# A decoder layer on one core of Trainium2: second buffers for eleven tiles, dummy matmuls at the start, and new orders and banks

## The reference

```python
# attention with positive random features, 16 heads of 16, 64 features a head
q, k, v = (split(x @ W.T + b) for W, b in ((Wq, bq), (Wk, bk), (Wv, bv)))
phi = lambda a: (exp(a @ orf.T / 16**0.25 - sum(a*a, -1) / (2*sqrt(16))) + 1e-6) / sqrt(64)
kv, ksum = phi(k).T @ v, sum(phi(k), tokens)
att = (phi(q) @ kv) / (phi(q) @ ksum)              # merged heads @ Wo.T + bo
x1 = layernorm(x + att)
# cross attention: 16 heads of 16, softmax between the context and x1, weights shared by the heads
x2 = layernorm(x1 + cross_attention(x1, ctx, Wq, Wk, Wv))
# feed-forward layer 256 -> 1024 -> 256, 8-bit activations and ternary weights
h = gelu(bitlinear(x2, w_gate)) * bitlinear(x2, w_up)
out = layernorm(x2 + bitlinear(h, w_down))
```

## Time and profile before

| what | value |
|---|---|
| median of 3 runs | 495.16 us (495.1 to 498.17) |
| the profiled execution | 495.66 us, its span from the first to the last instruction 493.6 us |
| busy: TensorE, VectorE, ScalarE, GpSimd | 447.2, 436.0, 429.1, 393.3 us (91, 88, 87, 80%) |
| mean granted TensorE clock | 0.977 of full speed |
| one tile in the full loop, 258.02 to 270.95 | 12.93 us, TensorE busy 12.93, ScalarE 12.85, VectorE 12.72, GpSimd 12.07 |

### The profile page before, as it was taken

The page is one execution under the profiler, slowest core; times in us unless marked ns, Lnnn a source line. Parts: engine busy times, 40 slices in busy tenths (PEclk is TensorE's granted clock), DMA queues, the critical chain, the costliest instruction groups (busy, mean ns, idle before and its releaser), DMA issues.

```text
span 493.6 us, 18532 instructions
## 1 busy us (share of the span) xinstructions
PE 447.2 (91%) x6598; PEld 305.1 (62%) x6598; DVE 436.0 (88%) x1286; ACT 429.1 (87%) x879; POOL 393.3 (80%) x885
## 2 busy tenths in 40 slices
PE   5588898999999999999999999999999999878752
PEld 3345666777666766777767677766766666554321
DVE  7755568999999999999999999999999999898771
ACT  3398988999999999999999999999999999776632
POOL 3379677889997898999999999999999897764533
PEclk9889999999999999999999999999999999997997
DMA  7848667777787587566666666666667676542122
GB/s 206 263 109 140 124 120 110 132 134 140 142 142 140 121 150 143 116 140 148 140 142 139 143 143 139 144 149 149 145 130 136 118 140 141 97 76 56 42 55 64
DMA packets 192660, 64.27 MB, mean 130 GB/s; under 512 B 172385, under 2 KB 192353, under 8 KB 192609
## 3 DMA queue, kind: packets, MB, share of 16 engines
q1 hardware_dynamic: 192432, 63.60, 64.2%
q10 hardware_dynamic: 176, 0.01, 0.0%
HBM read 17.31 MB, written 4.19 MB: 44 GB/s over the span
## 4 chain that ended last, share of the span: by engine, by line
PE 58%; DMA 11%; ACT 10%; DVE 9%; issue 5%; POOL 3%; SPq 3%; POOLq 0%; DVEq 0%; ACTq 0%
PE bank L1355 10%; PE bank L1741 8%; DMA tT<-pkT 5%; PE bank L1682 4%; PE bank L1543 4%; PE bank L1780 4%; PE bank L1453 3%; PE bank L1500 2%; PE bank L1719 2%; PE bank L1387 2%; PE bank L1392 2%; DVE hh L1101 2%; DMA pkAT<-pkA 2%; PE bank L1515 2%; PE bank L1571 2%
## 5 line engine op out<-in xcount | busy, mean ns | idle before, releaser
L1355 PE MATMUL bank<-wq_hi,xT 128*128 128x512 f16 (+1 forms) x256 | 73.2, 341 | 1.5 <-ACT xT L636 1.5
L516 POOL TENSOR_TENSOR rs<-ve,mhalf 128x1 f32<-128x1 f32 x96 | 53.2, 555 | 0.0
L1052 DVE TENSOR_REDUCE negm<-bank 128x4 f16<-128x512 f32 x64 | 42.9, 670 | 6.7 <-PE bank L1592 6.6
L1097 DVE SCALAR_TENSOR_TENSOR g<-th,bank 128x512 f32<-128x512 f32 x64 | 43.0, 675 | 4.7 <-ACT th L774 3.5
L750 ACT ACTIVATE pT<-bank 128x512 f32<-128x512 f32 x64 | 39.0, 610 | 8.0 <-PE bank L1672 6.9
L1355 PE MATMUL bank<-wq_lo,xT 128*128 128x256 f16 (+1 forms) x128 | 43.5, 340 | 0.0
L1053 DVE TENSOR_REDUCE negm<-bank 128x4 f16<-128x512 f32 x64 | 43.5, 679 | 0.0
L682 ACT ACTIVATE x<-y,nmr,rs 128x256 f32<-128x256 f32 x64 | 39.8, 623 | 3.6 <-DVE y L1158 2.9
L702 ACT ACTIVATE phq<-bank 128x512 f32<-128x512 f32 x64 | 39.7, 637 | 3.2 <-PE bank L1387 3.2
L1101 DVE TENSOR_TENSOR hh<-g,bank 128x512 f32<-128x512 f32 x64 | 42.4, 674 | 0.0
L1780 PE MATMUL bank<-downT,hqT 128*128 128x256 bf16 x256 | 33.2, 273 | 8.1 <-DMA hqT<-hq 8.1
(11 more groups left out here) (186 smaller groups left out, 1570.0 us busy)
## 6 DMA issues: line engine op xcount, KB each, us to landing
xs<-in_x_dram SPq DMA_DIRECT2D x32, 128.0 KB, 2.3
xr<-in_x_dram SPq DMA_DIRECT2D x32, 128.0 KB, 2.3
cs<-in_ctx_dram SPq DMA_DIRECT2D x32, 128.0 KB, 2.2
out_dram<-ot SPq DMA_DIRECT2D x32, 128.0 KB, 2.0
ffn_ld<-in_L_ffn_w_gate_dram SPq DMA_DIRECT2D x1, 1024.0 KB, 8.9
ffn_ld<-in_L_ffn_w_up_dram SPq DMA_DIRECT2D x1, 1024.0 KB, 6.4
ffn_ld<-in_L_ffn_w_down_dram SPq DMA_DIRECT2D x1, 1024.0 KB, 8.4
pkAT<-pkA SPq DMA_TRANSPOSE x64, 3.2
```

What stands on the lines that cost most here:

```text
L516: g.tensor_tensor(rs[n - 1][:, :], ve[n - 1][:, :], mhalf[:, :], ALU.pow).then_inc(done[f"pw{n}"], 1)
L1052: v.tensor_reduce(negm[:, 0, cols], even.rearrange("p (c t) -> p c t", c=4), AX, ALU.max, negate=True)
L1097: v.scalar_tensor_tensor(g1[:, n, :], th[:, n, :], 1.0, gate, ALU.add, ALU.mult).then_inc(done[f"gl{n}"], 1)
L1355: last = T.matmul(o, xT[:, 2 * part + c, :], w[:, c, cols], start=(n == 0), stop=(n == 5))
```

## The change

**Second buffers.** `xpk`, `xT`, `qk`, `pkA`, `pkAT`, `phk`, `x1T`, `pkT`, `pkC`, `hq` and `hqT` get a second SBUF buffer, indexed by the tile's parity. `th` and `g1` have no memory of their own any more: they lie in `wld`, which held the q, k, v and output weights at the start. The waits that kept one tile's writer off the other tile's reader are dropped, or reach one tile further back.

```diff
-        xpk = sb("xpk", [P, 2, D], F16)
-        xT = sb("xT", [P, 4, P], F16)
-        qk = sb("qk", [P, 2 * H, DK])
+        xpk = sb("xpk", [P, 2, 2, D], F16)
+        xT = sb("xT", [P, 2, 4, P], F16)
+        qk = sb("qk", [P, 2, 2 * H, DK])
...
-        th = sb("th", [P, 2, 512])
-        g1 = sb("g1", [P, 2, 512])
+        th = wld[:, 0:2, :, :].rearrange("p a b d -> p a (b d)")
+        g1 = wld[:, 2:4, :, :].rearrange("p a b d -> p a (b d)")
...
             def load_c(t, par):
-                wait(sp, "clo", t, -2)
...
             def qT(t, par):
-                wait_ahead(sp, t, par, ("lo", 0), ("phq0", -1))
...
             def kT(t, par):
-                wait_ahead(sp, t, par, ("lo", 0), ("nlo", 0), ("phk1", -1))
...
+                wait_ahead(sp, t, par, ("lo", 0), ("nlo", 0))
...
             def nhi(t, par):
-                wait_ahead(pool, t, par, ("nr", 0), landings=(("kT", -1), ("qT", -1),))
...
+                wait_ahead(pool, t, par, ("nr", 0))
```

```diff
+            def keep_busy(count):
+                for _ in range(count):
+                    T.matmul(at_qk[:, 0:P], idh[:, :], idh[:, :], start=True, stop=True)
+
+            keep_busy(18)
             for n in range(3):
                 transpose_weight(n, weight_banks[n])
+                if n == 1:
+                    keep_busy(8)
```

```diff
             def iteration(i, par):
                 go(load_c, i, par, 3)
                 go(load_x, i, par, 0)
-                go(store, i, par, 12)
                 go(cT_, i, par, 5)
-                go(qT, i, par, 2)
+                go(load_r, i, par, 4)
                 go(hqT_, i, par, 9)
                 go(row, i, par, 6)
                 go(kT, i, par, 2)
+                go(store, i, par, 11)
                 go(tT_, i, par, 5)
-                go(load_r, i, par, 3)
+                go(qT, i, par, 2)
```

More of the change, by code:

```diff
@@ L115, in decoder_kernel @@
         cs = sb("cs", [P, 2, D])
-        x1T = sb("x1T", [P, 2, P])
-        pkT = sb("pkT", [P, H, 4, DK], F16)
-        pkC = sb("pkC", [P, H, 4, DK], F16)
+        x1T = sb("x1T", [P, 2, 2, P])
+        pkT = sb("pkT", [P, 2, H, 4, DK], F16)
+        pkC = sb("pkC", [P, 2, H, 4, DK], F16)
         tT = sb("tT", [P, 2, PAIRS, P], F16)
@@ L880, in _ @@
+                trail(ephq1, i, -43, 28)
+                trail(x1_, i, -41, 26)
+                trail(th0, i, -38, 23)
+                trail(mT, i, -40, 25)
+                trail(x1T_, i, -41, 26)
+                trail(th1, i, -38, 23)
+                trail(hi, i, -45, 30)
+                trail(thi, i, -41, 26)
+                trail(vh, i, -40, 24)
+            run(act, ramp, iteration, drain, (-29, -14), 16, 30, (-16, -2))
         @block.vector
@@ L1354, in project @@
                     for part, w in ((0, wq_hi), (0, wq_lo), (1, wq_hi)):
-                        last = T.matmul(o, xT[:, 2 * part + c, :], w[:, c, cols], start=(n == 0), stop=(n == 5))
+                        last = T.matmul(o, xT[:, par, 2 * part + c, :], w[:, c, cols], start=(n == 0), stop=(n == 5))
                         n += 1
@@ L1778, in dn @@
+                only_at(pe, t, 26, "aT", 31)
+                wait_looped(pe, "aT", t, 5)
                 wait_moved(pe, "hqT", t, par)
                 for k in range(8):
-                    last = T.matmul(at_dn, hqT[:, k, :], downT[:, k, :], start=(k == 0), stop=(k == 7))
+                    last = T.matmul(at_dn, hqT[:, par, k, :], downT[:, k, :], start=(k == 0), stop=(k == 7))
                 last.then_inc(done["dn"], 1)
             def ramp(i):
-                if i == -18:
-                    pe.wait_ge(done["m1"], 2)
@@ new lines, in ramp @@
+                if i == -25:
+                    pe.wait_ge(prep_ev, 4)
+                once(ternaries[2], i, -25)
+                lead(nump, i, -27, 9)
+                lead(phk0, i, -28, 10)
+                lead(wo, i, -26, 8)
+                if i == -22:
+                    pe.wait_ge(done["p1"], 3)
+                once(ternaries[5], i, -22)
+                lead(phk1, i, -28, 10)
+                lead(ntp, i, -27, 9)
+                if i == -25:
+                    pe.wait_ge(done["xT"], 6)
@@ new lines, in ramp @@
+                once(ternaries[3], i, -25)
+                lead(pv1, i, -24, 6)
+                lead(pv0, i, -24, 6)
+                once(ffn_means, i, -28)
+                lead(s0, i, -25, 7)
+                lead(qkm, i, -30, 12)
+                lead(phq1, i, -28, 10)
+                lead(oxp, i, -24, 6)
+                lead(xqTp, i, -23, 5)
+                lead(phq0, i, -28, 10)
+                if i == -26:
+                    pe.wait_ge(done["ad1"], 1)
+                once(ternaries[1], i, -26)
@@ L1868, in keep_busy, with keep_busy_at @@
+            def keep_busy_at(i, at, count):
                 if i == at:
                     for _ in range(count):
-                        T.matmul(pb[0][:, :], idb[:, :], gateT[:, 0, 0:512], start=True, stop=True)
+                        T.matmul(pb[6][:, :], idb[:, :], gateT[:, 0, 0:512], start=True, stop=True)
             def drain(i):
-                if i == 2:
-                    pe.wait_ge(done["vh"], TILES)
-                    pe.wait_ge(done["tlo"], TILES)
-                    pe.wait_ge(done["thi"], TILES)
@@ new lines, in drain @@
+                keep_busy_at(i, -8, 13)
+                trail(st1, i, -40, 24)
+                trail(st0, i, -40, 24)
+                if i == -9:
+                    pe.wait_ge(done["m1"], 32)
+                keep_busy_at(i, -9, 3)
+                trail(kvp, i, -43, 27)
+                trail(wo, i, -42, 26)
+                trail(nump, i, -43, 27)
+                trail(phk1, i, -44, 28)
+                trail(phk0, i, -44, 28)
+            run(pe, ramp, iteration, drain, (-34, -17), 14, 30, (-16, -5))
```

1183 lines of the change are left out of this document (581 added, 602 removed).

## The result

The changed kernel took 491.77 us as the median of 3 runs (489.03 to 492.72), against 495.16 before. The ratio is 0.9893, with a 95% interval of 0.9858 to 0.9929. Run again in e1, it took 490.07 against 496.00: 0.9869 (0.9838 to 0.9900). Single executions of either kernel spread over 3 to 5 us, so a medians' difference of 1 us says little, and what follows leans on traces.

What follows compares the result with a forecast made beforehand. ScalarE was taken to set the pace after the start until TensorE fills, with the loop full on three engines. Terms −2.7 − 1.5 − 2.0 − 1.0 + 0.2 = −7.0 took 495.66 to 488.7 us, range 483.5 to 497.5.

Steps and rivals of the forecast that it cites:

- Start, −2.7: First tiles: new VectorE and load orders bring ScalarE's first phq earlier, taken as 2.7 us saved.
- the half-clock value of −2.1: Start: if tile 1's twelve matmuls run at half clock, phq0 comes at 25.2, 2.1 us earlier.
- Second buffers up to 90, −1.5 and −2.0: ScalarE's waits, 20 to 90 us: dropping those for pkAT saves 1.5 us, those for phq 2.0.
- 118 to 212, −1.0: Stage from 118 to 212 us: fewer SyncE waits ahead of tT cut TensorE's waiting, saving 1.0 us (0 to 2.7).
- The full stage, price 0: Loop from 212 to 350 us: TensorE busy 138.00 of 138, so dropped waits give nothing.
- My bound of −1.3: Full loop: if TensorE's busy time is partly stretched, ScalarE's floor allows at most 1.3 us saved over 18 tiles.
- Orders, +0.2: Loop chain from thi through tT to s0: new orders use up 0.8 us of slack, charged 0.2 us (0 to +4.8).
- Tail, 0: Last down projection: 18 dummies replace sixteen and still end before its transpose lands; no change, ends +0.3 and −0.5.
- all falls: Rival: start, waits, the stage to 212 and full loop all gain their most, −11.9, so 483.8 us; chance 0.15.
- the lead is lost again (2): Rival: transposes land only after three weight loads, the start gives nothing; 494.9 us; chance 0.25 with the buffers-do-nothing rival.
- tT's chain binds (3): Rival: the loop's thi, tlo, tT, s0 chain becomes the bound; 500.7 us at 0.75 a tile; chance 0.12.
- the buffers do nothing (4): Rival: TensorE is full wherever buffers would act, only the start moves; 493.0 us; chance 0.25 with the lost-lead rival.

Runs made afterwards that it cites:

- e1: The changed kernel run once more, nothing altered: 490.07 us, ratio 0.9869 to the kernel before.
- e2: The changed kernel with the kernel before's start orders on SyncE and VectorE: 493.30 us.
- e5: The kernel before with only the start orders changed (no second buffers, no start dummies, old banks): 500.68 us, ratio 1.0088.
- e10: The kernel before with the changed start orders and the output weight's load, transpose and copy moved behind the first tile: 500.46 us, ratio 1.0074.
- e6: The kernel before with only the eleven second buffers and the needless waits dropped: 494.70 us, ratio 0.9979.
- e9: The kernel before with a second buffer for qk alone: 496.30 us, ratio 1.0011.
- e4: The changed kernel without any of the 48 dummy matmuls in the drain: 492.70 us.
- e12: The changed kernel with 32 dummy matmuls in the drain, as before had them, instead of 48: 491.17 us, ratio 0.9882.
- e3: The changed kernel without the 26 dummy matmuls at the start: 491.00 us.
- e7: The changed kernel with ScalarE's hi moved back behind x2, one turn later, as before had it: 512.51 us, ratio 1.0328.
- e8: The changed kernel with tile 2's x load ahead of the up and down weight loads: 490.25 us.
- e11: The kernel before with the eleven second buffers, changed start orders and output weight's work behind the first tile; old banks and loop orders: 497.69 us, ratio 1.0019.

## Why the prediction was right, and where it was not

The forecast of 488.7 lies 3.1 under the first median and 1.4 under the second, in its range; the profiled execution, against which the sum was made, ended at 489.03. The sum of 7.0 against a measured 6.3 (by spans) is partly luck: the front was forecast at 6.2 and gave 2.6, and what made up for it is 0.7 in the full loop and 2.3 in the drain, neither of which the sum has.

- **Start, −2.7: right in its events,** and the half-clock value of −2.1 was the better one: phq at 25.13, forecast 25.2. Transposes at 17.75 (17.1, the gate sum starting at 14.12 and not 13.64) and the first phk at 21.37 (21.0) agree. What the orders are worth at the end is 1.3 (traces) to 3.2 (medians), by e2. What the step missed is that the term isn't the orders' alone. By e5 and e10 the same orders cost 4.5 us without the rest: in their traces the late x load, GpSimd's order and the single `qk` stand in the way, one behind the other, and no run takes away one of them alone. ScalarE's idle time from 0 to 30 fell by 1.7 us, where I had 2.6.
- **Second buffers up to 90, −1.5 and −2.0: wrong.** ScalarE's wait for pkAT is gone, as forecast, but its waits for phq became 2.5 us in 20 to 60 (0.6 before) and 1.3 in 60 to 90 (2.6 before; rows below), and the q/k of VectorE, 4.7 us ahead of before at tile 4 (40.26 against 44.98), is 2.1 ahead at tile 10 (115.82 against 117.91). The failed step is "Dropped waits are worth what ScalarE stood in them". In e6, with the buffers alone, there is no lead up to tile 7: the wait for pkAT is gone there too, and ScalarE stands 2.7 us for phq from 60 to 90, against 2.6 before. A removed wait let the next one come last. ScalarE's waits after, 20 to 60 and 60 to 90, which answer to the earlier trace rows:

```profile
ACT phq L699 <- PE bank L1385: 2.5, 2, 2.1
...
ACT phq L699 <- PE bank L1385: 1.3, 1, 1.3
```

- **118 to 212, −1.0: near.** The lead grows 0.7; TensorE's waits for tT fall from 2.0 to 0.9 us.
- **The full stage, price 0: wrong in its reason.** I read 138.00 of 138 as a bound, and e9 shows the same 138.00 at a period of 12.74. TensorE's busy time stretched to fill what there was. So did ScalarE's, which I gave as the floor: 12.85 a tile before, 12.67 in e9 (137.24 of 138, at 12.74). What the loop turned on was VectorE's q/k waiting for `lo` of the tile before, a wait of 1.2 us in six places over 212 to 350, that I passed over with the nine other doubled tiles, whose waits are those of "engines that aren't ScalarE". Dropping it alone takes 0.19 us a tile (e9). The changed kernel keeps only 0.06 of that (12.87): its orders or its banks, which no run parts, give 0.1 a tile back. 12.87 is under the 12.9 that I had named as the sign that TensorE's fullness was never the bound, and the sign was right. My bound of −1.3 holds the measured −0.7.
- **Orders, +0.2:** not seen. tT is issued at 266.37, lands 3.2 later, and s0 starts at 270.11, so 0.5 us of slack are left of 0.8.
- **Tail, 0: right for what it priced, and a stretch of 2.3 to 2.5 us left out.** From tile 28 to tile 31 nothing is gained (26.38 before, 26.49 after), and e4 shows that dummies as such are worth 2.6 us there, a worth which before, with 32 of its own, had as well. The gain lies between `ad3` of tile 21 and that of tile 28, about 370 to 460, ahead of nearly all dummies, a stretch for which my sum has no term. By the traces, with the granted clock between the two:

| trace | drain's orders and banks | tile 21 to 28 | clock |
|---|---|---|---|
| before | old | 87.93 us | 0.94 |
| e5, e10, e9 | old | 86.95, 86.46, 88.63 | 0.96, 0.98, 0.96 |
| changed, e1, e12 | new | 85.38, 86.00, 87.15 | 0.98, 1.00, 0.98 |
| e2, e3, e4, e7, e8 | new | 85.4 to 86.4 | 0.98 to 1.00 |
| e6, e11 | old, all second buffers | 83.94, 85.62 | 1.00, 1.00 |

With all second buffers the old orders and banks are at least as short there as the new ones, so the new ones aren't needed for this gain. And the profiled execution of before may have been a poor one in this stretch: with the same drain e5 and e10 took 1.0 and 1.5 us less at a higher clock, and e9 0.7 more. How much of the 2.5 is the buffers' and how much the clock's stays open, with one trace each.

The rivals: that all falls didn't happen. That the lead is lost again (2) didn't either, yet a part of its mechanism, the x load behind three weights, is what e5 and e10 suffered from. That tT's chain binds (3) had 0.5 us to spare. That the buffers do nothing (4) is wrong for the loop, and nearly right for the front. The one arrangement that did make the loop slower, e7, did it through GpSimd's queue, which I hadn't weighed at all.

## What to carry to other kernels

A busy share of 100% on TensorE is a bound only if the same work can't be seen to fit in less; look for a short wait that comes once a tile on any engine, 0.2 us will do, and price it before the long waits of the ramp. With orders written by hand, the parts of a change don't add: the start orders were worth 1.3 to 3.2 us with the rest in place and cost 4.5 without. Before moving an instruction, list what waits behind its consumers on every queue. Dummies placed by hand go with a timing: with before's dummies and another timing, tiles 28 to 31 took 28.5, 29.4 and 28.4 us (e6, e9, e11) against 26.4.

## What the runs showed of the hardware

- Dummy matmuls at the start put tile 0's twelve matmuls at the full clock in every trace that has them; without them tile 0's ran at half (e3). A matmul of 512 columns follows the one before by 0.43 us at half clock and by 0.22 at the full one. Whether tile 1's follow at the full clock isn't settled by the wait before them: after 2.24 us most ran at half in the first trace, after 2.14 to 3.06 us all ran at the full clock in e1, e4, e7, e8 and e12.
- In the drain the gaps without dummies cost 0.86 us on each four matmuls of 512 columns and on the eight of the down projection, 1.1 us a tile (e4). In e9, whose timing is another, before's dummies left the last tile's gate and up steps at 1.89 and 1.80 us and its down projection at 1.89.
- The same matmuls took TensorE 12.93 us of busy time a tile before and 12.74 in e9, all of the period each time; in two traces of the changed kernel at one period it was busy for 137.90 and 136.33 of 138 us.
- SyncE's issue of the down load took 5.62 us in the changed kernel, and 5.75 in e10, with 2 MB ahead of it; the changed kernel's other loads up to there took 0.4 to 0.8 each.
